# Macaron layer with a gated delta rule: POOL work moved to ScalarE, with new orders, stages and PSUM banks

## The chip, the core and the metric

The kernel runs on one core of one Trainium2 chip. The metric is the device time of one execution in microseconds. The engines are called PE (TensorE), DVE (VectorE), ACT (ScalarE), POOL (GpSimd) and SP (SyncE).

## What is computed

Input and output are 2 sequences of 4096 tokens with 256 channels, all float32. The layer is a feed-forward half step, a mixer, and the same feed-forward half step again:

```python
x = x + 0.5 * ffn(layernorm(x))
x = x + mixer(layernorm(x))
x = x + 0.5 * ffn(layernorm(x))

def ffn(x):                       # x_prev: the token before
    xr = mu_r * x + (1 - mu_r) * x_prev
    xk = mu_k * x + (1 - mu_k) * x_prev
    return sigmoid(xr @ W_r.T) * (square(relu(xk @ W_k.T)) @ W_v.T)

def mixer(h):                     # 16 heads of 16 channels
    q, k, v = (silu(conv4(h @ W.T)) for W in (Wq, Wk, Wv))
    q, k = l2norm(q) / 4, l2norm(k)
    beta, g = sigmoid(h @ Wb.T), -exp(A_log) * softplus(h @ Wa.T + dt_bias)
    for t in tokens:              # one 16x16 state per head
        S = S * exp(g[t])
        S = S + outer(k[t], (v[t] - k[t] @ S) * beta[t])
        o[t] = q[t] @ S
    return (rmsnorm(o) * norm_w * silu(h @ Wg.T)) @ Wo.T
```

## The kernel before

The 4096 tokens are cut into 32 groups of 128 tokens, both sequences together, so that a tile is 128 partitions by 512 columns. The recurrence is computed in chunks of 16 tokens: inside a chunk a triangular system is solved, and eight chunk steps (`chain`, n = 0 to 7) carry the state through a group.

The work of a group is split into some hundred segments, and a segment belongs to one engine. Each engine has its order of segments written out by hand in a loop `for step in range(GROUPS + 6)`, 38 steps. `on(segment, step - k)` runs a segment for group `step - k` if there is such a group, so that k is the stage at which the segment stands, and six to seven groups are in flight. An engine executes its list strictly in order; the engines wait for each other by semaphores. A segment of PE also waits until the PSUM bank that it writes is free. The table `PS` (L35) gives each product its bank, and the second to fourth `wait_ge` of a PE segment name the last reader of that bank.

The segments that matter here, with their lines:

- **DVE.** `stats1` to `stats3` (L1055, L1058) and `shift1` to `shift3` (L1241, L1187, L1319) belong to the layer norms. `mix_k1`, `mix_r1`, `mix_k3`, `mix_r3` mix a token with the one before (L1076, into XK and XR). `conv_q`, `conv_k`, `conv_v` (L1089) add three taps out of PSUM. `k_normed` (L1166) writes the normalised keys. `gram0` to `gram3` (L1346 to L1422) apply decays to Gram products and copy keys into KD (L1352, L1380, L1401, L1422). `solve_mul` and `solve_sub` (L1106, L1111) are the fifteen rows of the triangular solve, `t_turn` (L1147) turns the result. `chain` (L1127) copies the state out of PSUM, `o_turn` (L1135) and `o_merge` (L1141) collect outputs, `d_out0` to `d_out3` add products into Z2. `x1`, `x2`, `x3` (L1438 and L1439, L1269, L1174 and L1175) add to the residual.
- **PE.** `chain` (L408), `t_product`, `d_product0` to `3`, `gram0` to `3` (all through `pairs`, L251), the projections `q_proj`, `k_proj`, `v_proj` (L242) and `gate` (L476), `wo` and the feed-forward products (L226, L233), `turn1` to `turn3` (L219), `decay_steps` (L374), `decay_sums` (L418), `k_squares`, `o_squares` (L563, L571).
- **ACT.** Everything with a function table, and most copies out of PSUM. Functions come in two table sets; `ln_exp_set()` and `silu_set()` (L635, L638) load one, and each stands twice in a step. `exp_d` (L700) makes E from the sums of `decay_steps`; `t_out0`, `t_out1` (L852 to L862) write WP.
- **POOL.** Fourteen segments of whole-tile products and copies, among them `square1` and `square3` (L956, L960), `v_both` (L990), `q_slots` (L985), `t_start` (L1013), `q_decayed` (L979), `g_ident` (L951), `g_diag`, `e_mask` (L1017), `stat0`, `stat1`, `beta_diag`, `o_sum`, `gate_norm`.

Two examples, a segment with its waits and a piece of the order of POOL:

```python
def q_slots(g):
    pool.wait_ge(s["qe"], g + 1)
    if g:
        pool.wait_ge(s["mt"], 4 * g)
    tt(vw(GZ[:, :, C:], [2 * U, PACKS], [C, 2], [1, C]), vw(QE[:], [C, PACKS], [0, 2], [1, C]),
       vw(slot, [0, PACKS], [1, 2], [0, C]), ALU.mult).then_inc(s["qp"], 1)
...
    on(e_mask, step - 4)
    on(q_decayed, step - 4)
    on(q_slots, step - 4)
    on(g_ident, step - 4)
    on(t_start, step - 4)
```

Of the kernel before, what the change touches and what calls it, by code (L numbers as in the profile page):

```python
# [1589 lines left out]
```

## Time and profile before

| | us |
|---|---|
| median of 3 runs (lowest to highest) | 1776.21 (1775.66 to 1776.98) |
| the profiled execution | 1770.41 |
| its span, first to last instruction | 1768.4 |
| granted TensorE clock, mean, as a share of full | 0.913 |
| HBM read and written | 12.14 MB and 8.39 MB |

The page gives the busy time of each engine over the span. The trace behind it answers by line, by form, by stretch of time and by wait. Busy PE time includes time at a lower granted clock, and the idle time of an engine that isn't the bottleneck costs nothing. DMA is busy for a few per cent after the first slices.

### The profile page before, as it was taken

How to read it: one execution, taken by the hardware profiler on the slowest of the kernel's cores; microseconds unless marked ns; L12 is line 12 of the kernel's file. 1: busy time of each engine (PE TensorE's matmuls, PEld its weight loads, DVE VectorE, ACT ScalarE, POOL GpSimd, SP SyncE). 2: the span in 40 equal slices, each digit the busy share in tenths (PEclk: the TensorE clock that was granted, in tenths of full speed). 3: DMA queues.
4: the chain of work that ended last, by engine and by line, in shares of the span. 5: the costliest groups of instructions: out<-in, count | busy, mean ns of one | idle time of the engine just before them, and what ended most of it. 6: DMA issues, size and time to landing. Idle time of an engine off the chain costs nothing.

```text
span 1768.4 us, 92707 instructions
## 1 busy us (share of the span) xinstructions
PE 1519.7 (86%) x40960; PEld 1242.9 (70%) x40960; DVE 1530.0 (87%) x3975; ACT 1023.4 (58%) x1947; POOL 583.9 (33%) x453
## 2 busy tenths in 40 slices
PE   3878988988898898898988898898889888898875
PEld 2667776777777777777777777777777777776664
DVE  2889899889998988999999989989998999898662
ACT  6756566545656554656555566655565665556533
POOL 0333333234433323433333432423442333343301
PEclk8989999989998988998999899999898999898877
DMA  4000000000000000000000000000000000000000
GB/s 132 1 3 4 16 15 14 5 15 16 16 15 15 4 15 15 15 16 15 3 16 15 15 16 16 9 9 15 15 16 15 11 9 9 9 10 10 10 9 13
DMA packets 21839, 26.46 MB, mean 15 GB/s; under 512 B 2241, under 2 KB 20801, under 8 KB 21441
## 3 DMA queue, kind: packets, MB, share of 16 engines
q1 hardware_dynamic: 21440, 20.54, 3.6%
q8 instruction: 325, 5.32, 1.3%
q14 instruction: 74, 0.60, 0.1%
HBM read 12.14 MB, written 8.39 MB: 12 GB/s over the span
## 4 chain that ended last, share of the span: by engine, by line
DVE 46%; PE 31%; issue 14%; ACT 5%; DVEq 1%; POOL 1%; ACTq 0%; POOLq 0%
PE ps L233 11%; DVE CV L1089 6%; PE ps L242 5%; DVE XR L1076 4%; PE ps L251 4%; DVE TZ L1111 4%; PE ps L408 4%; DVE T L1147 3%; PE ps L476 3%; DVE KD L1352 3%; DVE st L1055 2%; DVE prod L1106 2%; DVE KD L1380 2%; ACT L635 2%; PE ps L392 2%
## 5 line engine op out<-in xcount | busy, mean ns | idle before, releaser
L408 PEld LDWEIGHTS ps<-MV,Z 32*32 32x32 f32 x16384 | 176.1, 112 | 192.6 <-DVE MV L1127 117.3
L408 PE MATMUL ps<-MV,Z 32*32 32x16 f32 x16384 | 203.2, 185 | 114.5 <-DVE MV L1127 96.3
L960 POOL TENSOR_TENSOR XK<-XK 128x512 f32<-128x512 f32 x32 | 38.9, 1215 | 635.3 <-ACT XK L799 635.3
L1089 DVE SCALAR_TENSOR_TENSOR CV<-ps,cw,CV 128x256 f32<-128x256 f32 x576 | 233.0, 475 | 5.9 <-ACT CV L681 5.9
L233 PE MATMUL ps<-w_v_ffn,XK 128*128 128x256 f32 x512 | 171.6, 493 | 4.2 <-DVE KD L1401 2.4
L251 PE MATMUL ps<-WP,KD 32*32 32x64 f32 x8192 | 148.4, 222 | 3.2 <-issue 2.0
L1111 DVE TENSOR_TENSOR TZ<-TZ,prod 128x30 f32<-128x30 f32 (+7 forms) x480 | 142.1, 296 | 6.9
L251 PEld LDWEIGHTS ps<-WP,KD 32*32 32x32 f32 x8192 | 128.9, 109 | 17.8 <-issue 13.0
L233 PEld LDWEIGHTS ps<-w_v_ffn,XK 128*128 128x128 f32 x512 | 119.1, 244 | 27.3 <-issue 3.0
L251 PEld LDWEIGHTS ps<-GK,T 32*32 32x32 f32 x8192 | 89.0, 108 | 69.2 <-issue 42.6
L251 PE MATMUL ps<-KQI,K 64*64 64x48 f32 x4096 | 133.2, 220 | 2.8 <-ACT K L632 2.7
L226 PE MATMUL ps<-XK,w_k_ffn 128*128 128x256 f32 x512 | 131.8, 403 | 2.5 <-DVE XK L1076 2.5
L233 PE MATMUL ps<-w_r_ffn,XR 128*128 128x256 f32 x512 | 128.6, 396 | 4.6 <-DVE XR L1076 3.3
L251 PEld LDWEIGHTS ps<-KQI,K 64*64 64x64 f32 x4096 | 125.1, 135 | 9.0 <-ACT K L632 2.8
L754 ACT ACTIVATE GS<-ps 128x512 f32<-128x512 f32 x32 | 19.1, 597 | 192.7 <-PE ps L476 192.6
L1106 DVE TENSOR_TENSOR prod<-A,TZ 128x30 f32<-128x30 f32 (+7 forms) x480 | 119.1, 248 | 10.1
L242 PE MATMUL ps<-YT,w_q 128*128 128x262 f32 x256 | 82.1, 475 | 49.8 <-DVE X L1175 49.8
L251 PE MATMUL ps<-GK,T 32*32 32x32 f32 x8192 | 106.0, 196 | 20.5 <-DVE T L1147 13.9
L1127 DVE COPY_PREDICATED MV<-pair,ps 128x128 f32<-128x128 uint32 x256 | 75.1, 293 | 50.9 <-PE ps L408 50.9
L233 PEld LDWEIGHTS ps<-w_r_ffn,XR 128*128 128x128 f32 x512 | 96.8, 199 | 17.2 <-DVE XR L1076 3.7
L226 PEld LDWEIGHTS ps<-XK,w_k_ffn 128*128 128x128 f32 x512 | 97.5, 200 | 15.9 <-issue 2.8
L1076 DVE SCALAR_TENSOR_TENSOR XR<-XR,mu,XT 128x256 f32<-128x256 f32 x128 | 108.3, 887 | 0.2 <-issue 0.2
(139 smaller groups left out, 3605.1 us busy)
## 6 DMA issues: line engine op xcount, KB each, us to landing
X<-in_x SPq DMA_DIRECT2D x32, 256.0 KB, 2.7
out_x<-X SPq DMA_DIRECT2D x32, 256.0 KB, 2.1
KQI<-in_blocks SPq DMA_DIRECT2D x2, 256.0 KB, 4.1
KD<-in_blocks SPq DMA_DIRECT2D x2, 256.0 KB, 4.6
w_r_ffn<-in_wT_r_ffn SPq DMA_DIRECT2D x1, 256.0 KB, 3.3
w_k_ffn<-in_wT_k_ffn SPq DMA_DIRECT2D x1, 256.0 KB, 3.6
w_v_ffn<-in_wT_v_ffn SPq DMA_DIRECT2D x1, 256.0 KB, 4.4
w_k<-in_wT_k SPq DMA_DIRECT2D x1, 256.0 KB, 4.3
```

What stands on the lines that cost most here:

```text
L226: last = mm(ps[:, dst * BANK + m * HB:dst * BANK + (m + 1) * HB], wt[:, k, m * P:(m + 1) * P], src[:, k * HB:(k + 1) * HB], start=(k == 0) ...
L233: last = mm(ps[:, dst * BANK + b * H:dst * BANK + (b + 1) * H], src[:, k * HB + b * TG:k * HB + (b + 1) * TG], wt[:, k, :], start=(k == 0) ...
L242: last = mm(ps[:, o:o + B * (CT + TG)], wt[:, k, m * P:(m + 1) * P], YT[:, k].rearrange("p b t -> p (b t)"), start=(k == 0), stop=(k == M ...
L251: last = mm(ps[rows, o:o + n], stat[rows, pk].rearrange("p s c -> p (s c)"), mov[rows], **flags)
L408: last = mm(ps[rows, o:o + C], Z2[g % 2][rows, pk, ab * U:(ab + 1) * U], MV[g % 2][rows, pk, ab, :], start=True, stop=True)
L476: last = mm(ps[:, o:o + HB], w["g"][:, k, m * P:(m + 1) * P], YT[:, k, :, CT:], start=(k == 0), stop=(k == M - 1))
L1076: last = stt(d3[:, rows], diff[:, rows], mu[:, kind, m:m + 1], XT[f][:, rows, 0:TG], ALU.mult, ALU.add)
L1089: stt(d4[:, m], src, cw[:, i, m, tap:tap + 1], d4[:, m], ALU.mult, ALU.add).then_inc(signal, 1)
L1106: tt(pr, a_j, t_j, ALU.mult).then_inc(s["sol"], 1)
L1111: tt(t_i, t_i, pr, ALU.subtract).then_inc(s["sol"], 1)
L1127: nc.vector.copy_predicated(state_rows_of(dst, m), vw(state_rows, [0, M * B], [1, U]), vw(src, [U, M * B], [1, U])).then_inc(s["ch_s"], 1)
L1147: nc.vector.transpose(vw(T2[:], [C, 2], [1, C], [U, PACKS]), vw(TZ[:], [2 * C * C, 2], [1, C], [C, U])).then_inc(s["tp"], 1)
```

## The change

Five segments move from POOL to ACT: `square1`, `square3`, `q_slots` (now two copies scaled by a mask column), `v_both` and `t_start`. The order of segments is written anew on PE, ACT, POOL and DVE, and many segments stand at another stage. Every product has its PSUM bank chosen anew, and the waits for banks on PE follow. ACT loads a table set six times per step. The arithmetic stays the same.

```diff
--- before.py
+++ after.py
@@ -32,9 +32,9 @@
 PAIR = U + 2 + HT + U
 AB0 = 320
 SOL = 2 * (C - 1)
-PS = {"xt1": 3, "yt": 0, "xt3": 0, "r1": 4, "k1": 6, "v1": 6, "r3": 0, "k3": 6, "v3": 5, "wo": 4, "g": 5,
-      "dd": 4, "eq": 1, "ssk": 3, "oss": 0, "gr0": 3, "d0": 1, "gr1": 1, "d1": 1, "gr2": 6, "d2": 1,
-      "gr3": 5, "d3": 0, "t0": 1, "t1": 6, "kc0": 3, "kc1": 4, "qc0": 5, "qc1": 2, "vc0": 2, "vc1": 4,
+PS = {"xt1": 4, "yt": 2, "xt3": 4, "r1": 3, "k1": 4, "v1": 4, "r3": 2, "k3": 3, "v3": 3, "wo": 1, "g": 6,
+      "dd": 3, "eq": 6, "ssk": 1, "oss": 4, "gr0": 6, "d0": 1, "gr1": 0, "d1": 6, "gr2": 4, "d2": 0,
+      "gr3": 6, "d3": 4, "t0": 4, "t1": 5, "kc0": 0, "kc1": 2, "qc0": 1, "qc1": 6, "vc0": 0, "vc1": 5,
       "ch": 7}
 
...
 def wo(g):
     pe.wait_ge(s["ot"], g + 1)
-    if g < GROUPS - 3:
-        pe.wait_ge(s["ck"], 6 * g + 24)
-        pe.wait_ge(s["tapk"], g + 4)
-    if g == GROUPS - 3:
-        pe.wait_ge(s["cv"], 6 * g + 18)
-        pe.wait_ge(s["tapv"], g + 3)
-    if g == GROUPS - 2:
-        pe.wait_ge(s["e"], g + 2)
+    if g < GROUPS - 1:
+        pe.wait_ge(s["mt"], 4 * g + 5)
     if g == GROUPS - 1:
         pe.wait_ge(s["x2"], g)
...
@@ q_proj @@
         pe.wait_ge(s["mix_in"], 16 * (len(MIX_IN) + 9))
     pe.wait_ge(s["yt"], g + 1)
     if g:
-        pe.wait_ge(s["cv"], 6 * g)
-        pe.wait_ge(s["tapv"], g)
-    if 1 <= g < 4:
         pe.wait_ge(s["gs"], g)
-    if g >= 4:
-        pe.wait_ge(s["x3"], g - 3)
+        pe.wait_ge(s["rnk"], g)
     conv_cols((PS["qc0"], PS["qc1"]), w["q"])
...
+def square1(g):
+    act.wait_ge(s["relu1"], g + 1)
+    af(KA[0][:], KA[0][:], ACT.Square).then_inc(s["ka1"], 1)
+
+def square3(g):
+    act.wait_ge(s["relu3"], g + 1)
+    af(KA[1][:], KA[1][:], ACT.Square).then_inc(s["ka3"], 1)
+
+def q_slots(g):
+    act.wait_ge(s["qe"], g + 1)
+    if g:
+        act.wait_ge(s["mt"], 4 * g)
+    own.done(af(GZ[:, :, C:2 * C], packs(QE[:]), ACT.Copy, scale=slot[:, 0:1]))
+    af(GZ[:, :, 2 * C:3 * C], packs(QE[:]), ACT.Copy, scale=slot[:, 1:2]).then_inc(s["qp"], 1)
+
+def v_both(g):
+    act.wait_ge(s["vt"], g + 1)
+    nc.scalar.copy(MV[g % 2][:, :, 1, :], MV[g % 2][:, :, 0, :]).then_inc(s["v2"], 1)
+
+def t_start(g):
+    if g == 0:
+        act.wait_ge(s["mix_in"], 16 * (len(MIX_IN) + 9))
+    if g:
+        act.wait_ge(s["tp"], g)
+    nc.scalar.copy(vw(TZ[:], [3 * C * C, 2], [1, C * C]),
+                   vw(t_one[:], [C * C, 2], [1, C * C])).then_inc(s["t_one_in"], 1)
+
```

The orders after the change, in short: `chain.2-5` is `on(chain, step - 5, 2)`, `mul` and `sub` are `solve_mul` and `solve_sub`.

```
PE: chain.2-5 k_squares-3 turn3-6 chain.3-5 v_proj-3 chain.4-5 turn1-1 turn2-2 chain.5-5 ffn3_k-6 chain.6-5 q_proj-2
  chain.7-5 ffn3_r-6 t_product.0-4 t_product.1-4 ffn3_v-6 t_product.2-4 t_product.3-4 k_proj-2 t_product.4-4
  t_product.5-4 t_product.6-4 o_squares-5 decay_sums-3 d_product0-4 t_product.7-4 ffn1_k-1 d_product1-4 d_product2-4
  decay_steps-3 gram0-3 d_product3-4 gram1-3 wo-5 gram2-3 chain.0-4 gram3-3 ffn1_r-1 chain.1-4 ffn1_v-1 gate-2
ACT: tap_q-3 o_square-6 norm1-1 t_out0-5 gates_wide-4 tap_k-3 ln_exp_set() o_root-6 halo3-6 exp_q-4 t_out1-5
  soft_exp-3 t_start-4 relu1-2 square1-2 v_both-5 exp_d-4 silu_set() silu_k-3 halo1-1 silu_v-4 square_k-3 ln_exp_set()
  rstd3-6 silu_set() silu_q-3 tanh1-2 q_slots-4 norm3-6 gate-3 ln_exp_set() rstd2-2 xt3-6 norm2-2 k_root-3 halo_y-2
  rstd1-0 yt-2 relu3-6 tap_v-3 square3-6 xt1-1 square_q-3 k_slots-3 o_first-5 silu_set() tanh3-6
POOL: g_ident-5 o_sum-6 stat0-4 stat1-4 q_decayed-4 gate_norm-6 g_diag-4 e_mask-4 beta_diag-3
DVE: d_out0-5 d_out1-5 d_out2-5 soft_low-3 o_norm-6 stats1-0 g_reduce-4 d_out3-5 gram0-4 chain.7-6 gram1-4 v_turn-4
  x2-6 gram2-4 stats3-6 chain.0-5 gram3-4 shift3-6 a_turn-4 chain.1-5 mul.0-4 o_turn.0-5 sub.0-4
  mul.1-4 sub.1-4 mul.2-4 soft_part-3 sub.2-4 x1-2 mul.3-4 sub.3-4 mul.4-4
  chain.2-5 sub.4-4 stats2-2 mul.5-4 sub.5-4 mul.6-4 chain.3-5 sub.6-4 o_turn.1-5
  mul.7-4 shift2-2 sub.7-4 mix_k3-6 chain.4-5 mul.8-4 sub.8-4 mul.9-4 sub.9-4
  o_turn.2-5 mul.10-4 chain.5-5 sub.10-4 soft_log-3 mul.11-4 sub.11-4 mul.12-4
  k_normed-3 sub.12-4 mul.13-4 chain.6-5 mix_r3-6 shift1-0 soft_max-3 sub.13-4 mul.14-4
  gates-3 sub.14-4 t_turn-4 o_turn.3-5 conv_v-3 o_merge-5 mix_k1-1 conv_q-2 gates_in-2 mix_r1-1 conv_k-2 x3-6
```

## Rows read from the trace of the kernel before

**Rows 1.** The page's busy time, share of the span and instructions of each engine.

```profile
PE 1519.7 (86%) x40960; PEld 1242.9 (70%) x40960; DVE 1530.0 (87%) x3975; ACT 1023.4 (58%) x1947; POOL 583.9 (33%) x453
```

**Rows 2.** Stretch 400 to 1400 us: time; PE, PEld, DVE, ACT, POOL busy; clock; DMA share; GB/s.

```profile
400.00:1400.00 1000.00, 891.53 (x24399) 731.07 (x24397) 917.84 (x2360) 588.76 (x1145) 351.31 (x269) 0.93 0.05 13
```

**Rows 3.** Line L1439 in that stretch: duration ns min/median/max, first and last start us.

```profile
L1439 DVE SCALAR_TENSOR_TENSOR X<-XR,X x19: 691/692/694, 439.2 to 1386.6; 128x512 f32<-128x512 f32 x19
```

**Rows 4.** Groups by form, DVE: operation xcount | busy us, mean ns | idle before.

```profile
L1076 DVE SCALAR_TENSOR_TENSOR XR<-XR,mu,XT 128x256 f32<-128x256 f32 x128 | 108.3, 887 | 0.2 <-issue 0.2
...
L1076 DVE SCALAR_TENSOR_TENSOR XK<-XR,mu,XT 128x256 f32<-128x256 f32 x128 | 57.2, 488 | 2.3
...
L1166 DVE TENSOR_TENSOR KQI<-CV,SK 128x512 f32<-128x512 f32 x32 | 50.5, 1577 | 0.0
L1352 DVE COPY_PREDICATED KD<-pair,KE 128x256 f32<-128x256 uint32 x32 | 48.7, 1523 | 0.0
L1380 DVE COPY_PREDICATED KD<-pair,KE 128x256 f32<-128x256 uint32 x32 | 42.3, 1323 | 0.0
...
L1319 DVE SCALAR_TENSOR_TENSOR nmr<-mv,rstd 128x2 f32<-128x2 f32 x32 | 35.6, 1112 | 0.6 <-ACT rstd L627 0.6
...
L1422 DVE COPY_PREDICATED KD<-pair,KE 128x256 f32<-128x256 uint32 x32 | 13.9, 435 | 0.0
...
L1241 DVE SCALAR_TENSOR_TENSOR nmr<-mv,rstd 128x2 f32<-128x2 f32 x32 | 5.7, 179 | 14.8 <-ACT rstd L627 14.8
```

**Rows 5.** Timeline, 848 to 852 us, DVE and POOL: start us, us, engine, line, operation.

```profile
848.14 1.26 POOL L979 TENSOR_TENSOR QE<-KQI,EQ 128x512 f32<-128x512 f32 x1
848.20 1.22 DVE L1319 SCALAR_TENSOR_TENSOR nmr<-mv,rstd 128x2 f32<-128x2 f32 x1
...
849.48 1.89 POOL L985 TENSOR_TENSOR GZ<-QE,pair 128x1024 f32<-128x1024 f32 x1
...
850.08 1.60 DVE L1352 COPY_PREDICATED KD<-pair,KE 128x256 f32<-128x256 uint32 x1
```

**Rows 6.** Waits from 400 to 1400 us: who waited for whom, total us, times, longest us.

```profile
PE ps L408 <- DVE MV L1127: 57.8, 19, 3.3
...
PE ps L242 <- DVE X L1175: 36.2, 19, 2.0
...
DVE MV L1127 <- PE ps L408: 24.1, 14, 1.9
```

**Rows 7.** Stretch 804 to 806.5 us, columns as in the second group.

```profile
804.00:806.50 2.50, 2.50 (x7) 1.55 (x5) 1.78 (x5) 0.00 (x0) 0.00 (x0) 0.50 0.00 0
```

**Rows 8.** Timeline of PE, then DVE, 800 to 852 us; in brackets the idle time before.

```profile
802.85 3.78 PE L233 MATMUL ps<-w_v_ffn,XK 128*128 128x256 f32 x8
...
807.68 0.30 DVE L1127 COPY_PREDICATED MV<-pair,ps 128x128 f32<-128x128 uint32 x1 [1.87 <-PE ps L408]
...
824.72 1.99 PE L233 MATMUL ps<-w_v_ffn,XK 128*128 128x256 f32 x8
```

**Rows 9.** Groups by form, POOL: the five operations that leave it, xcount | busy us, mean ns.

```profile
L985 POOL TENSOR_TENSOR GZ<-QE,pair 128x1024 f32<-128x1024 f32 x32 | 60.8, 1899 | 2.5
...
L960 POOL TENSOR_TENSOR XK<-XK 128x512 f32<-128x512 f32 x32 | 38.9, 1215 | 635.3 <-ACT XK L799 635.3
L956 POOL TENSOR_TENSOR XK<-XK 128x512 f32<-128x512 f32 x32 | 38.5, 1204 | 39.4 <-ACT XK L722 39.4
L1013 POOL COPY TZ<-t_one 128x512 f32<-128x512 f32 x32 | 25.8, 805 | 0.0
L990 POOL COPY MV<-MV 128x512 f32<-128x512 f32 x32 | 19.5, 609 | 96.5 <-DVE MV L1445 96.5
```

**Rows 10.** Groups by form, ACT: table loads of one set, a square, a masked copy out of PSUM.

```profile
L635 ACT ACT_TABLE_LOAD x77 | 98.8, 1283 | 1.9 <-DVE prod L1455 0.6
...
L861 ACT ACTIVATE WP<-ps,pair 128x512 f32<-128x512 f32 x32 | 21.9, 685 | 64.8 <-PE ps L251 64.8
...
L786 ACT ACTIVATE SK<-CV 128x512 f32<-128x512 f32 x32 | 19.7, 614 | 0.2
```

More of the change, by code:

```diff
@@ L447, in turn3 @@
                     pe.wait_ge(s["ro"], g + 1)
+                if g < GROUPS - 4:
+                    pe.wait_ge(s["x1"], g + 5)
                 turn(PS["xt3"], XN[2], s["xt3_ps"])
@@ L575, in _ @@
             for step in range(GROUPS + 6):
-                on(chain, step - 5, 0)
+                on(chain, step - 5, 2)
+                on(k_squares, step - 3)
                 on(turn3, step - 6)
-                on(ffn1_r, step - 2)
-                on(chain, step - 5, 1)
-                on(ffn1_v, step - 2)
-                on(chain, step - 5, 2)
-                on(gate, step - 3)
                 on(chain, step - 5, 3)
+                on(v_proj, step - 3)
+                on(chain, step - 5, 4)
                 on(turn1, step - 1)
-                on(ffn3_r, step - 6)
-                on(chain, step - 5, 4)
-                on(v_proj, step - 3)
+                on(turn2, step - 2)
                 on(chain, step - 5, 5)
@@ L912, in _ @@
                 on(o_root, step - 6)
-                on(k_slots, step - 4)
+                on(halo3, step - 6)
+                on(exp_q, step - 4)
                 on(t_out1, step - 5)
-                on(tap_q, step - 3)
+                on(soft_exp, step - 3)
+                on(t_start, step - 4)
+                on(relu1, step - 2)
+                on(square1, step - 2)
+                on(v_both, step - 5)
+                on(exp_d, step - 4)
+                silu_set()
+                on(silu_k, step - 3)
                 on(halo1, step - 1)
-                on(exp_d, step - 4)
-                on(rstd1, step - 1)
+                on(silu_v, step - 4)
+                on(square_k, step - 3)
+                ln_exp_set()
                 on(rstd3, step - 6)
-                on(norm3, step - 6)
-                on(xt3, step - 6)
-                on(soft_exp, step - 3)
                 silu_set()
@@ L1027, in _ @@
             for step in range(GROUPS + 6):
-                on(square1, step - 2)
+                on(g_ident, step - 5)
+                on(o_sum, step - 6)
+                on(stat0, step - 4)
+                on(stat1, step - 4)
+                on(q_decayed, step - 4)
                 on(gate_norm, step - 6)
-                on(v_both, step - 4)
+                on(g_diag, step - 4)
                 on(e_mask, step - 4)
-                on(q_decayed, step - 4)
-                on(q_slots, step - 4)
-                on(g_ident, step - 4)
-                on(t_start, step - 4)
-                on(square3, step - 6)
-                on(g_diag, step - 3)
-                on(stat0, step - 3)
-                on(o_sum, step - 5)
                 on(beta_diag, step - 3)
-                on(stat1, step - 3)
         @block.vector
@@ L1458, in _ @@
             for step in range(GROUPS + 6):
-                on(g_reduce, step - 4)
-                on(d_out1, step - 5)
-                on(gates_in, step - 3)
+                on(d_out0, step - 5)
+                on(d_out1, step - 5)
+                on(d_out2, step - 5)
+                on(soft_low, step - 3)
+                on(o_norm, step - 6)
+                on(stats1, step)
+                on(g_reduce, step - 4)
+                on(d_out3, step - 5)
+                on(gram0, step - 4)
+                on(chain, step - 6, 7)
+                on(gram1, step - 4)
+                on(v_turn, step - 4)
                 on(x2, step - 6)
-                on(conv_q, step - 3)
-                on(d_out2, step - 5)
+                on(gram2, step - 4)
                 on(stats3, step - 6)
-                on(d_out3, step - 5)
-                on(shift3, step - 6)
-                on(gram0, step - 4)
-                on(gram1, step - 4)
-                on(gram2, step - 4)
-                on(shift1, step - 1)
-                on(gram3, step - 4)
                 if step == 5:
```

328 lines of the change are left out of this document (165 added, 163 removed).

## The prediction

> **What bounds the kernel now.** I read the page's busy shares first [rows 1]: DVE and PE are both near 87%, ACT at 58%, POOL at 33%. A share over the whole span hides fill and drain, so next comes the steady stretch [rows 2] and its period. One DVE line runs once for each group of tokens; it started 19 times from 439.2 to 1386.6 us [rows 3], so the period is 947.4 / 18 = 52.6 us. In 1000 us there are 19.0 periods. Per period [rows 2] DVE is busy 917.84 / 19 = 48.3 us, PE 46.9, ACT 31.0, POOL 18.5. DVE idles only 4.3 us. It is the bound, with PE close behind.
>
> How much of the 48.3 us is work? The by-form groups answer it [rows 4]: instructions of one shape have very different means. The second copy into KD takes 1323 ns where the fourth, the same shape, takes 435. The timeline shows why [rows 5]: a DVE shift of 2 columns starts 0.06 us after a POOL product, takes 1.22 us, and ends as that product does. The next KD copy starts inside POOL's 1.89 us masked copy and ends just after it. So some DVE instructions stand still until POOL's current instruction is done. Those hit read two SBUF tensors. The price of it [rows 4]: mix of XR 128 x (887 - 488) = 51.1 us; normalised keys 32 x (1577 - 692) = 28.3, taking 692 from a 512-wide line that is never hit [rows 3]; KD copies 32 x (1523 - 435) + 32 x (1323 - 435) = 63.2; shift 32 x (1112 - 179) = 29.9. Sum 172.5 us, 5.4 per group. DVE's own work is then 48.3 - 5.4 = 42.9 us.
>
> The waits close the picture [rows 6]. Once a period PE waits up to 3.3 us for the chain's copy on DVE, which is late because the stretch before it (decayed Gram products) holds the blocked KD copies and shift. A second wait, up to 2.0 us, is that of the query projection for the residual sum on DVE. After the first wait the granted clock is 0.50, the 1.2 GHz level [rows 7]: the same eight matmuls take 3.78 us where they take 1.99 later, and DVE then idles 1.87 us at the next chain copy [rows 8]. That is how 4.3 us of DVE idle arise: lost time on DVE makes PE wait, the wait costs PE its clock, and DVE waits in turn.
>
> **The change part by part.** *Leaves POOL:* masked query copies 1899 ns, squares 1204 and 1215, start rows 805, second values 609 [rows 9], together 5.7 us per group, so POOL goes from 18.5 to 12.8. What DVE gets back depends on which of its instructions POOL meets. In proportion, 5.4 x 12.8 / 18.5 = 3.7 us stay, 1.7 are saved. Bounds: 1 us stays if the new order keeps POOL under single-input work, 6 if every remaining instruction blocks something.
>
> By the new lists POOL's decay products and g_ident come behind beta_diag, which is released by gates, while DVE runs t_turn and conv_v (one SBUF tensor in each); e_mask stays just ahead of gram0; and nothing of POOL is due during gram0 to gram3, where 2.9 us of the 5.4 were lost (KD copies 63.2 us and shift 29.9 over 32). Against that, beta_diag now meets the end of the solve, o_sum meets mix_k1, and stat0 and stat1 meet mix_r1: three or four meetings of about 1.2 us. Both readings give some 3.7 us, and I take it. DVE: 42.9 + 3.7 = 46.6 us per period.
>
> *Arrives at ACT:* two squares at 614 ns, two masked copies at 685, two plain copies at about 614 [rows 10]: 3.8 us. ACT also gets six table loads per step in place of four. Now one of the two lines that load shows 77 = 2 x 38 + 1 of 1283 ns [rows 10], the other one has as many but the one at the start; two more per step are 2.6 us, 76 x 1283 ns = 97.5 us in all. ACT goes from 31.0 to 37.4 us of the period. It is not the bound; this stands beside DVE work and I cost it at nothing. If the cover goes (a period under 38 us, or a wait queued ahead of exp_d) it costs what it lacks.
>
> The Trainium skill (ScalarE: Activation LUTs, section "Table sets: the hidden batching unit") reckons a switch of table set at about 2.7 us; by that the 76 more loads would be an estimated 205 us and ACT some 40 us per period, still below DVE. The trace's duration is half of it and decides.
>
> *New PSUM banks and order:* no instruction is added or removed on PE or DVE. The new waits fall mostly on work of an earlier group. The query projection leaves its place behind x3 and now follows chain step 6 and waits for gs and rnk of the group before, so the second PE wait has no cause left. The first has: chain step 0 still needs d_out3, and step 1 the copy of step 0, with gram3 and ffn1_r between. Behind it now stand ffn1_v and gate, two blocks of about 2 us that at the lower clock take 3.8 each [rows 8]. DVE has about 4 us of its own between its copies 1 and 2 (an estimate: x1 with two lines of some 692 ns, an output transpose and ten short solve steps). So an idle of up to some 2.6 us can return at chain copy 2. DVE idle now 4.3; bounds 0.5 (PE never cold) to 5 (cold as now, longer blocks); I take 2.0, the old 4.3 less the part behind the projection.
>
> *Sum.* Period 46.6 + 2.0 = 48.6 us, 4.0 less. Of 38 steps 27 have every stage; the thin ones together I count as one more: 28 x 4.0 = 113 us. The profiled execution took 1770.4 us, 5.8 less than the 1776.2 median of the runs. 1776.2 - 113 = **1663 us**. Its own range, with period 47.1 to 50.1, is 1621 to 1706.
>
> **Rivals.**
>
> *A. The blocking nearly vanishes.* DVE 42.9 + 1.5 and 1.6 idle give 46.0; PE must fit: 46.9 us busy at a mean clock of 0.93 [rows 2] is about 43.2 at full clock (14% of the time at half). 28 x 6.6 = 185 us, 1591. For: gram0 to gram3 are free of POOL. Against: three meetings remain, and PE and DVE with 43 us each leave little play. 0.13.
>
> *B. The blocking only moves.* The rows show that whichever starts first runs to its end, and the other one waits. Then removing 5.7 us of POOL work need not free a proportionate share: a POOL instruction released just ahead of a two-input DVE instruction costs its full length. With 4.7 of the 5.4 us left and the longer cold blocks keeping idle at 3.9, the period is 42.9 + 4.7 + 3.9 = 51.5: 28 x 1.1 = 31 us, 1745. 0.18. The Trainium skill says the same (SBUF — State Buffer, section "Who interferes with whom"): a DVE instruction with two SBUF inputs and a GpSimd one that reads SBUF exclude each other for a whole instruction, by issue order. By that rule, the trace agrees: 1.22 us for a shift of 2 columns.
>
> *C. Slower: ACT becomes the late one at exp_d.* On its in-order list exp_d now stands behind a table load, o_root, exp_q, t_out1, soft_exp, t_start, relu1, square1 and v_both. t_out1 waits for the last triangular product. From its start to exp_d are at least 2 x 685 + 4 x 614 ns = 3.8 us, soft_exp's five small steps not counted, where before it stood behind t_out1, tap_q and halo1 only. Behind it wait e_mask, then gram0 on DVE with the whole chain. It decides from the point where ACT reaches exp_d more than about 1 us after decay_steps; then POOL's e_mask and what follows also slide back under the Gram stretch. Price: blocking back at 5.4 us, idle 2.0 + 3.7: 42.9 + 5.4 + 5.7 = 54.0, 28 x 1.4 = 39 us more, 1815. For: ACT rises by 6.4 us and each table load holds all behind it. Against: ACT still has 11 us to spare at 48.6, and decay_steps too has moved ahead of the Gram products. 0.15.
>
> *D. Nothing changes,* gains and losses cancel within 0.2% (about what a measurement of this kernel can tell from no change): 1776. 0.03.
>
> **How the numbers follow.** Forecast 0.51, A 0.13, B 0.18, C 0.15, D 0.03. Faster by over 0.2%: 0.51 + 0.13 + 0.18 = 0.82. Same 0.03, slower 0.15. The range runs from A's value to that of no change, 1590 to 1776: half of A's chance lies below it and most of C's above, together 2 in 10.
>
> **What would show it.** In the profile of the changed kernel: the period, from the starts of x1's last line, near 48.6; POOL busy about 583.9 - 183.5 = 400 us, no POOL instruction inside gram0 to gram3; all four KD copies near 435 ns; the shift near 180; XR mix still above 488; the query projection without a wait for DVE; 153 + 76 = 229 table loads; ACT busy about 1240 us; clock above 0.93. The prediction is wrong if KD copies stay above 1 us (B), if DVE waits at gram0 for POOL's E behind ACT's exp_d (C), or if PE stays above 2.4 us of waits per period for the chain copy with ffn1_v and gate at the low clock.

## The result and the profile after

The changed kernel takes 1549.05 us (median of 4 runs, 1546.72 to 1550.92); the kernel before took 1776.6 (median of 4 beside them, 1775.66 to 1792.74). The ratio on record is 0.87, 95% interval 0.8649 to 0.8751; the quotient of the two medians, 0.872, lies inside it. That is 227.6 us less, where 113 were forecast. The time lies 41 us below the lower end of the range.

The page's busy times and shares of the span (1548.8 us) answer to [rows 1]:

```profile
PE 1443.1 (93%) x40960; PEld 1183.5 (76%) x40960; DVE 1383.2 (89%) x3975; ACT 1219.2 (79%) x2215; POOL 396.9 (26%) x293
```

A stretch of whole periods answers to [rows 2], same columns (time; PE, PEld, DVE, ACT, POOL busy; clock):

```profile
401.20:1294.10 892.90, 882.46 (x25602) 725.56 (x25601) 863.32 (x2481) 728.29 (x1361) 247.90 (x180) 1.00 0.05 16
```

The line that gave the period [rows 3] is L1453 now:

```profile
L1453 DVE SCALAR_TENSOR_TENSOR X<-XR,X x21: 691/692/693, 401.2 to 1294.1; 128x512 f32<-128x512 f32 x21
```

It started 21 times in 892.9 us: the period is 892.9 / 20 = 44.65 us, 8.0 less than 52.6, where 4.0 less was forecast. The count of periods held: 28 x 8.0 = 224 us of the 227.6. Per period PE is busy 882.46 / 20 = 44.1 us, DVE 43.2, ACT 36.4, POOL 12.4. PE has 0.5 us to spare and its granted clock is 1.00: PE, no longer DVE, is the fullest engine, and it loses no clock in the steady stretch. Below, e4 shows that DVE stands right behind it.

The waits of PE in the stretch 400 to 1300 us (total, times, longest) hold no wait for the chain copy nor for the residual sum, which were 3.3 and 2.0 us at the longest [rows 6]. The longest that another engine causes is 0.4 us, once:

```profile
PE ps L418 <- DVE Z L1316: 0.4, 1, 0.4
```

The two blocks behind the chain steps, `ffn1_v` and `gate`, run at full clock, where `ffn1_v` took 3.78 us before [rows 8]:

```profile
709.42 1.99 PE L233 MATMUL ps<-w_v_ffn,XK 128*128 128x256 f32 x8
711.25 1.89 PE L480 MATMUL ps<-YT,w_g 128*128 128x256 f32 x8
```

The DVE groups by form (busy us, mean ns, over the whole run) answer to [rows 4]. The second KD copy (L1394) fell from 1323 to 437 ns, the first from 1523 to 478, the shift from 1112 to 153, the keys from 1577 to 692. The mix of XR only went from 887 to 731, and the mix of XK rose from 488 to 699:

```profile
L1090 DVE SCALAR_TENSOR_TENSOR XR<-XR,mu,XT 128x256 f32<-128x256 f32 x128 | 88.5, 731 | 0.1
L1090 DVE SCALAR_TENSOR_TENSOR XK<-XR,mu,XT 128x256 f32<-128x256 f32 x128 | 84.2, 699 | 2.3
...
L1180 DVE TENSOR_TENSOR KQI<-CV,SK 128x512 f32<-128x512 f32 x32 | 22.1, 692 | 2.5 <-ACT SK L849 2.3 <-issue 0.3
...
L1366 DVE COPY_PREDICATED KD<-pair,KE 128x256 f32<-128x256 uint32 x32 | 15.3, 478 | 0.0
...
L1394 DVE COPY_PREDICATED KD<-pair,KE 128x256 f32<-128x256 uint32 x32 | 14.0, 437 | 0.0
...
L1125 DVE TENSOR_TENSOR TZ<-TZ,prod 128x30 f32<-128x30 f32 x64 | 11.7, 183 | 0.1
...
L1333 DVE SCALAR_TENSOR_TENSOR nmr<-mv,rstd 128x2 f32<-128x2 f32 x32 | 4.9, 153 | 1.0 <-ACT rstd L638 1.0
```

The timeline of POOL and DVE over one period (start, us) shows where POOL's work stands now. Ahead of `beta_diag` (724.98) POOL is idle for 24.15 us, over the whole Gram stretch; its list goes on while DVE convolves, and then meets both mixes:

```profile
724.98 1.06 POOL L1022 TENSOR_TENSOR LD<-cz,msk 128x512 f32<-128x512 f32 x1 [24.15 <-DVE cz L1233]
...
730.99 1.96 DVE L1090 SCALAR_TENSOR_TENSOR XK<-XR,mu,XT 128x256 f32<-128x256 f32 x2
...
731.40 1.27 POOL L1002 TENSOR_TENSOR OSQ<-OSQ,SQ 128x512 f32<-128x512 f32 x1 [3.43 <-ACT OSQ L843]
...
735.41 1.61 POOL L1033 TENSOR_TENSOR ST<-ST,LD 128x512 f32<-128x512 f32 x1
735.42 1.88 DVE L1090 SCALAR_TENSOR_TENSOR XR<-XR,mu,XT 128x256 f32<-128x256 f32 x2
```

`o_sum` starts inside the mix of XK, and `stat1` starts 0.01 us before the mix of XR. ACT's table loads in the steps stand under two lines, 229 in all (one more comes ahead of the steps):

```profile
L649 ACT ACT_TABLE_LOAD x115 | 147.5, 1283 | 2.5 <-DVE prod L1469 0.6
L646 ACT ACT_TABLE_LOAD x114 | 146.3, 1283 | 2.0
```

### The profile page after: what moved, and what is told of

It is laid out like the page before. It is cut to its first block, busy times and chain, and to the rows that moved or that the text cites. A ratio compares the mean times of both kernels' runs of the same rounds, so it can differ in the third digit from the quotient of the medians.

```text
span 1548.8 us, 92755 instructions
## 1 busy us (share of the span) xinstructions
PE 1443.1 (93%) x40960; PEld 1183.5 (76%) x40960; DVE 1383.2 (89%) x3975; ACT 1219.2 (79%) x2215; POOL 396.9 (26%) x293
## 4 chain that ended last, share of the span: by engine, by line
issue 72%; POOL 21%; ACT 3%; PE 2%; DVE 1%; POOLq 0%; ACTq 0%; DVEq 0%
POOL GZ L996 4%; POOL GD L1042 3%; POOL OSQ L1002 3%; POOL ST L1033 3%; POOL E L1036 3%; POOL ST L1028 3%; POOL GS L1009 2%; ACT L649 1%; ACT L646 1%; PE ps L226 0%; PE ps L242 0%; POOL QE L1016 0%; PE ps L233 0%; POOL LD L1022 0%; PE ps L251 0%
## 5 line engine op out<-in xcount | busy, mean ns | idle before, releaser
L1022 POOL TENSOR_TENSOR LD<-cz,msk 128x512 f32<-128x512 f32 x32 | 33.9, 1060 | 815.5 <-DVE cz L1233 815.5
L404 PEld LDWEIGHTS ps<-MV,Z 32*32 32x32 f32 x16384 | 164.9, 107 | 75.2 <-issue 55.5
L404 PE MATMUL ps<-MV,Z 32*32 32x16 f32 x16384 | 190.4, 181 | 18.1 <-DVE MV L1141 9.2
L251 PE MATMUL ps<-KQI,K 64*64 64x48 f32 x4096 | 148.1, 221 | 4.4 <-issue 3.4
L649 ACT ACT_TABLE_LOAD x115 | 147.5, 1283 | 2.5 <-DVE prod L1469 0.6
L646 ACT ACT_TABLE_LOAD x114 | 146.3, 1283 | 2.0
L251 PE MATMUL ps<-WP,KD 32*32 32x64 f32 x8192 | 138.6, 215 | 6.8 <-issue 5.6
L636 ACT ACTIVATE lnv<-mv,headp 128x2 f32<-128x2 f32 x96 | 28.3, 294 | 131.5 <-DVE mv L1072 131.5
L233 PE MATMUL ps<-w_v_ffn,XK 128*128 128x256 f32 x512 | 127.2, 391 | 0.4 <-ACT XK L910 0.4
L1125 DVE TENSOR_TENSOR TZ<-TZ,prod 128x30 f32<-128x30 f32 (+7 forms) x480 | 119.8, 250 | 6.9
L233 PEld LDWEIGHTS ps<-w_v_ffn,XK 128*128 128x128 f32 x512 | 92.2, 189 | 13.1 <-ACT XK L910 0.8
L251 PE MATMUL ps<-GK,T 32*32 32x32 f32 x8192 | 96.9, 194 | 3.8 <-issue 2.1
L1141 DVE COPY_PREDICATED MV<-pair,ps 128x128 f32<-128x128 uint32 x256 | 74.1, 289 | 19.4 <-PE ps L404 18.5
```

The lines of the kernel that those rows point to most:

```text
L233: last = mm(ps[:, dst * BANK + b * H:dst * BANK + (b + 1) * H], src[:, k * HB + b * TG:k * HB + (b + 1) * TG], wt[:, k, :], start=(k == 0) ...
L251: last = mm(ps[rows, o:o + n], stat[rows, pk].rearrange("p s c -> p (s c)"), mov[rows], **flags)
L404: last = mm(ps[rows, o:o + C], Z2[g % 2][rows, pk, ab * U:(ab + 1) * U], MV[g % 2][rows, pk, ab, :], start=True, stop=True)
L646: nc.scalar.preload_act_table_set("natural_log_exp_and_others")
L649: nc.scalar.preload_act_table_set("silu_and_others")
L1125: tt(t_i, t_i, pr, ALU.subtract).then_inc(s["sol"], 1)
```

## The experiments

Two things had to be told apart. First, what took the time: POOL blocking DVE instructions that read two SBUF tensors, or late POOL results, or the order. Second, why the period fell by twice the forecast. The table gives each run per period, in us: the busy share of the stretch 400 to 1300 us times the period. A count over whole periods, as the text uses in places, differs by up to 0.3; DVE of the kernel before is such a count. The last column is the ratio on record to the kernel before run beside it (medians there 1773.7 to 1778.5).

| kernel | period | PE busy | DVE busy | ACT busy | POOL busy | clock | median us | ratio (95%) |
|---|---|---|---|---|---|---|---|---|
| before | 52.6 | 46.9 | 48.2 | 31.1 | 18.5 | 0.93 | 1776.6 | 1 |
| changed | 44.65 | 44.1 | 43.2 | 36.4 | 12.3 | 1.00 | 1549.05 | 0.870 (0.865 to 0.875) |
| e1 before, POOL one column | 44.2 | 43.5 | 41.3 | 30.9 | 1.7 | 1.00 | 1534.95 | 0.865 (0.861 to 0.868) |
| e13 changed, POOL one column | 44.5 | 44.0 | 41.0 | 36.3 | 0.8 | 1.00 | 1543.10 | 0.869 (0.863 to 0.875) |
| e9 before, POOL fills only | 44.5 | 43.5 | 41.8 | 30.9 | 15.1 | 1.00 | 1548.70 | 0.873 (0.867 to 0.879) |
| e2 before, five segments moved | 47.6 | 44.7 | 44.8 | 34.2 | 12.0 | 0.98 | 1640.96 | 0.924 (0.919 to 0.928) |
| e15 before, `q_slots` moved | 50.7 | 45.9 | 47.1 | 32.1 | 16.1 | 0.95 | 1713.43 | 0.965 (0.959 to 0.972) |
| e3 changed, segments back on POOL | 46.4 | 44.6 | 45.0 | 33.1 | 17.5 | 1.00 | 1599.43 | 0.900 (0.896 to 0.905) |
| e8 before, POOL's list alone | 47.2 | 43.9 | 45.4 | 30.8 | 17.8 | 1.00 | 1638.89 | 0.925 (0.921 to 0.930) |
| e10 before, e2 and a list like e8's | 49.0 | 44.9 | 46.9 | 34.3 | 12.3 | 0.98 | 1679.32 | 0.945 (0.940 to 0.951) |
| e7 before, more PE work | 50.9 | 46.7 | 48.1 | 30.7 | 18.5 | 0.97 | 1724.87 | 0.973 (0.967 to 0.980) |
| e4 changed, less PE work | 44.3 | 43.4 | 42.9 | 36.3 | 12.4 | 1.00 | 1544.31 | 0.870 (0.866 to 0.873) |
| e5 changed, 2 POOL products, Gram | 44.7 | 44.2 | 43.3 | 36.4 | 14.3 | 1.00 | 1548.46 | 0.874 (0.870 to 0.878) |
| e11 changed, 4 POOL products, Gram | 44.5 | 44.0 | 43.3 | 36.4 | 16.6 | 1.00 | 1547.66 | 0.871 (0.866 to 0.876) |
| e6 changed, 2 POOL products, conv | 44.8 | 44.1 | 43.2 | 36.4 | 14.3 | 1.00 | 1555.03 | 0.878 (0.874 to 0.881) |
| e12 changed, 4 POOL products, conv | 49.0 | 45.9 | 45.3 | 36.4 | 17.3 | 0.95 | 1672.62 | 0.942 (0.936 to 0.947) |
| e14 changed, 2 more table loads | 46.4 | 44.7 | 43.6 | 39.0 | 12.1 | 0.99 | 1608.99 | 0.906 (0.898 to 0.914) |

### What POOL's work costs

**e1** keeps every wait and signal of POOL in the kernel before. From group 2 on it leaves the computation of POOL's products and of its copy of the values out and sets one column in the place of each; `t_start` stays. The heart of the edit:

```diff
-            tt = nc.gpsimd.tensor_tensor
+            full = nc.gpsimd.tensor_tensor
...
+            def tiny():
+                used[0] += 1
+                return nc.gpsimd.memset(few[:, used[0]:used[0] + 1], 0.0)
+
+            def tt(dst, a, b, op):
+                if now[0] < 2:
+                    return full(dst, a, b, op)
+                return tiny()
```

> The kernel before with every tensor product of POOL, and its copy of the values, replaced from group 2 on by the setting of one column, each under the waits and signals it had (t_start stays). It leaves that part of the computation out. Theory 1, the blocking of two-input DVE instructions and what follows from it (PE waits, low clock, DVE idle) is the whole difference between the two kernels: the period falls from 52.6 us to 45 or 46, 1776 - 28 x 7 = 1580 us, all four KD copies near 435 ns, clock above 0.96. Theory 2, the new order is what counts: only the 5 to 6 us of blocking go and the waits of PE stay, half of it or less reaches the period: 1690 us or more.

Measured: 1534.95 us, 45 below what theory 1 expected, and the old order with PE at full clock. The stretch of 19 periods:

```profile
440.50:1279.70 839.20, 827.13 (x24368) 685.23 (x24356) 784.54 (x2357) 584.62 (x1142) 32.20 (x266) 1.00 0.05 16
```

DVE's own work is 784.54 / 19 = 41.3 us, against 866.75 / 18 = 48.2 in the kernel before: POOL's blocking was 6.9 us a period. The rows below are DVE's by form over whole steady periods, first of the kernel before, then of e1:

```profile
L1076 DVE SCALAR_TENSOR_TENSOR XR<-XR,mu,XT 128x256 f32<-128x256 f32 x72 | 64.0, 929 | 0.0
...
L1166 DVE TENSOR_TENSOR KQI<-CV,SK 128x512 f32<-128x512 f32 x18 | 31.4, 1742 | 0.0
...
L1352 DVE COPY_PREDICATED KD<-pair,KE 128x256 f32<-128x256 uint32 x18 | 28.9, 1607 | 0.0
L1380 DVE COPY_PREDICATED KD<-pair,KE 128x256 f32<-128x256 uint32 x18 | 23.9, 1330 | 0.0
L1111 DVE TENSOR_TENSOR TZ<-TZ,prod 128x30 f32<-128x30 f32 x36 | 22.4, 622 | 0.0
L1319 DVE SCALAR_TENSOR_TENSOR nmr<-mv,rstd 128x2 f32<-128x2 f32 x18 | 21.7, 1205 | 0.0
```

```profile
L1097 DVE SCALAR_TENSOR_TENSOR XR<-XR,mu,XT 128x256 f32<-128x256 f32 x76 | 33.3, 481 | 0.0
...
L1187 DVE TENSOR_TENSOR KQI<-CV,SK 128x512 f32<-128x512 f32 x19 | 13.2, 693 | 0.0
...
L1373 DVE COPY_PREDICATED KD<-pair,KE 128x256 f32<-128x256 uint32 x19 | 8.4, 442 | 0.0
...
L1132 DVE TENSOR_TENSOR TZ<-TZ,prod 128x30 f32<-128x30 f32 x38 | 7.4, 194 | 0.0
```

XR mix 4 x (929 - 481) = 1.8 us, KD copies 1.2 + 0.9, shift 1.05 (its mean in e1 is 154 ns), keys 1.05, and the last `sub` of the solve 2 x (622 - 194) = 0.85: 6.8 of the 6.9.

**e13** is the same edit on the changed kernel.

> The changed kernel with every POOL product from group 2 on replaced by the setting of one column (that part of the computation is left out). DVE's blocking, 1.9 us a group by now, goes. Theory 1, PE at full clock is the floor of both kernels: the time is that of the old order without blocking, 1530 to 1545 us. Theory 2, the 1.9 us that are left still cost their length: 1549 - 28 x 1.9 = 1496 us.

```profile
400.00:1300.00 900.00, 888.38 (x25889) 734.79 (x25888) 829.06 (x2512) 734.51 (x1376) 17.00 (x180) 1.00 0.05 16
```

1543.10 us, against 1549.05: the intervals of the two ratios overlap almost wholly, so this is theory 1. DVE falls from 870.01 to 829.06 us, over whole periods by 2.1 us per period, and the period goes from 44.65 to 44.5 only, with PE busy 44.0 of it. The blocking left in the changed kernel is both mixes, 4 x (750 - 477) and 4 x (736 - 482) = 2.1 us, by its own steady rows and e13's:

```profile
L1090 DVE SCALAR_TENSOR_TENSOR XR<-XR,mu,XT 128x256 f32<-128x256 f32 x80 | 56.8, 750 | 0.0
L1090 DVE SCALAR_TENSOR_TENSOR XK<-XR,mu,XT 128x256 f32<-128x256 f32 x80 | 55.6, 736 | 1.4
```

```profile
L1111 DVE SCALAR_TENSOR_TENSOR XK<-XR,mu,XT 128x256 f32<-128x256 f32 x80 | 35.2, 482 | 1.4
...
L1111 DVE SCALAR_TENSOR_TENSOR XR<-XR,mu,XT 128x256 f32<-128x256 f32 x80 | 34.9, 477 | 0.0
```

**e9** asks whether it is POOL's being busy, or late, that costs, or its reads. From group 2 on each product becomes a fill of about its length and a fill of one column, which read nothing, and the copy of the values a shorter fill; that part of the computation is left out. The heart of the edit, with a function `fill` that two others call:

```diff
+            def fill(cols):
...
+                nc.gpsimd.memset(few[k % 3][:, 0:cols], 0.0).then_inc(s["fills"], 1)
+                return nc.gpsimd.memset(tick[:, k:k + 1], 0.0)
+
+            def tt(dst, a, b, op):
+                if now[0] < 2:
+                    return full(dst, a, b, op)
+                return fill(1280)
```

> The kernel before with every tensor product of POOL, from group 2 on, replaced by a fill of 1280 columns of a spare tile (about 1.2 us by the 0.95 us of the 1024-column fill at the start) and a one-column fill, its copy of the values by a shorter fill; waits and signals stay. It leaves that part of the computation out. POOL is then busy nearly as long as before but reads nothing from SBUF. Theory 1, DVE's two-input instructions wait because POOL reads SBUF: they run free and the time is that of the run with tiny POOL work, 1535 to 1560 us. Theory 2, that run was faster because POOL's results came sooner (latency of e_mask, stat1, o_sum): the time stays at 1700 or more. Theory 3, writing blocks too: KD copies above 1 us, 1740 or more.

1548.70 us with POOL busy 15.1 us per period, where it was 18.5. The timeline shows copies into KD taking 0.45 and 0.44 us though a fill of some 1.16 us starts inside each of them (at 699.71 and 700.85), and, in the same stretch, one that takes 0.86 us because POOL's only operation that still reads SBUF (the start rows) began 0.05 us before it:

```profile
699.61 0.45 DVE L1378 COPY_PREDICATED KD<-pair,KE 128x256 f32<-128x256 uint32 x1
699.71 1.16 POOL L955 MEMSET few<- 128x1280 f32 x1
...
700.83 0.44 DVE L1406 COPY_PREDICATED KD<-pair,KE 128x256 f32<-128x256 uint32 x1
...
701.99 0.61 POOL L1039 COPY TZ<-t_one 128x512 f32<-128x512 f32 x1
702.04 0.86 DVE L1427 COPY_PREDICATED KD<-pair,KE 128x256 f32<-128x256 uint32 x1
```

The time lies 14 us above that of e1, with ratios whose intervals overlap, and DVE is still busy 0.4 us longer per period than in e1, since the start rows go on reading. So POOL results that come late are at most a small part of the 228 us; POOL's reads are the cause. The Trainium skill (SBUF — State Buffer, section "Who interferes with whom") says that a DVE instruction with two SBUF inputs contends with a GpSimd one that reads SBUF and not with one that only writes it: these rows agree.

### Moves against places

**e2** puts the five segments on ACT in the kernel before, with its orders and banks kept (added lines of ACT's list, the comments are mine):

```diff
+                on(square1, step - 2)   # ACT, behind relu1
+                on(v_both, step - 4)    # behind t_out1
+                on(t_start, step - 4)
+                on(q_slots, step - 4)   # behind soft_exp
+                on(square3, step - 6)   # behind relu3
```

> The kernel before in its own order and banks, with only the five segments moved from POOL to ACT (squares behind their relus, v_both and t_start behind t_out1, q_slots behind soft_exp), four table loads as before. Theory 1: the Gram stretch of DVE still has POOL's e_mask, q_decayed and g_ident on top of it, so some 2 to 3 us of blocking a period go (the KD copies that met q_slots and t_start, squares on mixes): 1776 - 28 x 2.5 = 1706 us, between 1680 and 1740. Theory 2, the moves bring the gain: below 1620. Theory 3, they bring nothing without the order: 1765 or more.

**e3** does the opposite: the changed kernel with the five segments back on POOL, `t_start` and `v_both` behind `o_sum`, `square1`, `q_slots` and `square3` behind `e_mask`.

> The changed kernel in its new order and banks, with the five segments back on POOL (t_start and v_both behind o_sum; square1, q_slots and square3 behind e_mask, thus under the Gram stretch of DVE), six table loads kept. Theory 1, place of POOL's work: square1 and q_slots (1.2 and 1.9 us) block KD copies again, the chain is late, PE waits and loses its clock: period from 44.7 to 48 or 49, 1549 + 28 x 4 = 1660 us, 1630 to 1700. Theory 2, the order alone is the gain: 1549 to 1565.

**e8** leaves every operation on POOL and changes three places of its list:

```diff
                 on(v_both, step - 4)
+                on(q_decayed, step - 4)
                 on(e_mask, step - 4)
-                on(q_decayed, step - 4)
-                on(q_slots, step - 4)
-                on(g_ident, step - 4)
                 on(t_start, step - 4)
                 on(square3, step - 6)
+                on(g_ident, step - 4)
+                on(q_slots, step - 4)
```

> The kernel before with all its POOL work, banks and other orders, only three POOL segments moved within POOL's own list: q_decayed ahead of e_mask, g_ident and q_slots behind square3 (which waits for relu3 and so starts at the end of the solve). Theory 1: the KD copies and the third shift are free, about 3 us of blocking and its knock-on go, while the later POOL list meets mixes and keys: 1776 - 28 x 4 = 1664 us, 1620 to 1700. If the moves to ACT were needed for any gain: 1765 or more.

Against the medians beside them, the moves alone (e2) give 138 us (ratio 0.924), the new orders, stages and banks alone, with the six table loads, (e3) 179 (0.900), both 228 (0.870). I had expected less of either, 1706 and 1660 us. The two don't add up: both take blocking away, and with the blocking gone e1 and e13 stop at 44.2 and 44.5 us. e8 is the surprise: with 17.8 us of POOL work per period it takes 135 us off, about as much as e2 with 12.0. Over the run its first two KD copies take 532 and 491 ns, the shift 493, the keys 792; only the mix of XR is left at 874. What matters is which DVE instruction POOL's list meets, not how much POOL does. In e3 the first KD copy meets `q_slots` and takes 1707 ns (mean over the run), longer than before's 1523, and the period is still 6 us shorter.

**e10** joins e2 with the places of e8 (`q_decayed` ahead of `e_mask`, `g_ident` released near the end of the solve).

> The old orders and banks with both cures: the five segments on ACT, and in POOL's list q_decayed ahead of e_mask and g_ident held until the end of the triangular solve. All of the computation is there. Alone the moves gave 1641 and the new places 1639 us. Theory 1, both only take blocking away and PE at full clock is the floor (43.5 to 44.1 us a period): 1776 - 28 x 7 = 1580 us, 1555 to 1600. Theory 2, the new order of PE, DVE and ACT and the banks hold a gain of their own: 1620 or more here, against 1549.

It takes 1679.32 us, worse than either, and theory 1 is refuted. The timeline (brackets: idle before) shows why. `g_ident` starts 0.21 us before the mix's difference, which then takes 2.31 us (685 ns in e1), `g_diag` holds the mix of XK, `stat0` holds a step of the solve (1.27 us), and PE waits 2.05 us for XK:

```profile
726.06 1.97 POOL L984 TENSOR_TENSOR GZ<-pair,EQ 128x1024 f32<-128x1024 f32 x1 [20.65 <-DVE TZ L1118]
...
726.27 2.31 DVE L1291 TENSOR_TENSOR XR<-XT 128x512 f32<-128x512 f32 x1
...
728.61 1.89 DVE L1083 SCALAR_TENSOR_TENSOR XK<-XR,mu,XT 128x256 f32<-128x256 f32 x2
...
728.87 1.35 POOL L1035 TENSOR_TENSOR GD<-EQ,msk 128x512 f32<-128x512 f32 x1 [0.84 <-ACT EQ L708]
...
730.55 3.68 PE L226 MATMUL ps<-XK,w_k_ffn 128*128 128x256 f32 x8 [2.05 <-DVE XK L1083]
```

Theory 2 had given 1620 or more, for a gain that the new orders hold of their own. With e1 and e13 beside it, that gain is in what POOL's list meets, and no other is to be seen.

**e15** moves only `q_slots`, behind `soft_exp` on ACT.

> The kernel before with only the masked query copies moved to ACT (behind soft_exp). Theory 1, the 1.9 us POOL product under the Gram stretch is the most harmful of the five: g_ident and t_start come 1.9 us sooner and end before the later KD copies, some 1 to 2 us of blocking go: about 1776 - 28 x 2 = 1720 us, 1690 to 1745, more than half of what all five moves gave (1641). If each move counts by its own length (1.9 of 5.7 us): 1776 - 135 x 0.33 = 1731 us; no more than 1765 if it is the squares that count.

It gains 61 us (1713.43), less than half of the 138 of all five moves, where I had expected more than half. The second KD copy falls from 1323 to 521 ns over the run, DVE by 1.1 us per period and the period by 1.95: each microsecond of blocking was worth nearly two here.

### Why a microsecond of DVE is worth more than one

**e7** adds to the kernel before: the matmuls of `ffn1_r` are issued twice, which puts 1.9 us of PE work ahead of PE's wait for the chain copy.

```diff
+                for b in range(B):
+                    for k in range(M):
+                        mm(ps[:, PS["r1"] * BANK + b * H:PS["r1"] * BANK + (b + 1) * H],
+                           XR[0][:, k * HB + b * TG:k * HB + (b + 1) * TG], w["r_ffn"][:, k, :], start=(k == 0), stop=(k == M - 1))
                 rows_out(PS["r1"], w["r_ffn"], XR[0], s["r1_ps"])
```

> The kernel before with the r product of the first feed-forward (8 matmul passes, 1.9 us) computed twice in a row on PE, ahead of the wait for the chain's copy, where PE idles 3.3 us a period. It adds work and computes the same. If the low clock after that wait is part of the knock-on: PE idles only 1.4 us there, ffn1_v takes 2.0 us and not 3.8, DVE does not idle at the next copy, and in spite of more work the kernel gets faster: 1776 - 28 x 1.5 = 1734 us, 1700 to 1765. If the clock costs nothing because PE has slack: 1774 to 1780 us, or more by up to 28 x 1.9 = 53 us if the added work isn't covered.

With more work the kernel takes 1724.87 us, 2.7% less than before. DVE's busy time is the same, 48.1 us. PE's timeline shows the chain step behind a wait of 1.60 us where it was up to 3.3, and then `ffn1_v` in 1.99 us where it took 3.78 [rows 8]:

```profile
734.53 0.73 PE L408 MATMUL ps<-MV,Z 32*32 32x16 f32 x64 [1.60 <-DVE MV L1131]
735.18 1.99 PE L233 MATMUL ps<-w_v_ffn,XK 128*128 128x256 f32 x8
```

The added work only fills time in which PE was idle, so the gain of 49 us is that of the clock: the half clock behind PE's wait was on the path, and it was worth about a fifth of the 228 us.

**e4** leaves out half of the `gate` product on the changed kernel (`for k in range(1)`).

> The changed kernel with the second half of the gate product left out on PE (4 of 8 matmul passes, 0.95 us a group). If PE at full clock (44.1 us busy of a 44.65 us period) is now the bound, with DVE busy 43.2 behind it: the period falls by 0.5 to 0.9 us, 1549 - 28 x 0.7 = 1529 us, 1520 to 1536. If DVE or ACT sets the period and PE only fills it: no change, 1546 to 1552.

PE's work falls by 0.7 us and the period by 0.3, where I had expected 0.5 to 0.9 or nothing; the ratio, 0.870, is the same. So PE is not the only limit: with 0.7 us taken off PE, or 2.1 off DVE (e13), the other one holds the period. That the two share the bound is argued from these runs; no run takes from both at once. ACT's list has little play as well, as e14 will show.

### What play the changed kernel has left

**e5**, **e11**, **e6** and **e12** add POOL products that read SBUF and that nobody waits for (`tt(DUM[i], t_one, t_one, mult)`, some 1.1 us each): two and four behind `e_mask`, under the Gram products; two and four behind `beta_diag`, ahead of `g_ident` (e5 with e11, e6 with e12).

> The changed kernel plus two POOL products a group (each 512 columns, SBUF in, SBUF out, 1.27 us, result unused), placed right behind e_mask, so that they fall under gram0 and gram1 of DVE. Theory 1, the place of POOL's work sets the price: the first KD copies wait 1.5 to 2 us a group, DVE's busy time rises by as much, and nothing covers it: 44.65 -> 46.2 to 47 us, 1549 + 28 x 1.9 = 1602 us, 1585 to 1620. Theory 2, POOL's work beside a full PE costs nothing: 1549 to 1555.

> The changed kernel with four added POOL products a group behind e_mask in place of two (1.02 us each as the last run showed, where both were over before the second KD copy). Now they reach over gram0 to gram2. Theory 1: the first three KD copies wait 0.3 to 1 us each, 1.5 to 2.5 us a group, DVE goes to about 45 us of work: 1549 + 28 x 1.5 = 1591 us, 1570 to 1615. Theory 2: no more than 1555.

> The same two POOL products, placed behind beta_diag instead, so that they fall under t_turn and conv_v of DVE, which read one SBUF tensor each. Theory 1: no DVE instruction waits for them, 1549 to 1556 us. If the amount of POOL's work counts and not its place: the same 1600 us as in the run with them under the Gram stretch.

> The same four products behind beta_diag, under t_turn and conv_v. DVE's instructions there read one SBUF tensor. They also hold g_ident and o_sum back by up to 4 us, which the list covers for the most part: Theory 1: 1555 to 1575 us, less than with the four under the Gram stretch. If the amount and not the place counts: the same as there.

Neither two nor four products in the Gram stretch cost anything (e5 1548.46 us, e11 1547.66), where theory 1 had 1602 and 1591. The four run from 700.10 to 704.58, yet of the KD copies inside them the first takes 0.73 us and the second 0.43 (means over the run 721 and 435 ns):

```profile
700.10 4.48 POOL L1048 TENSOR_TENSOR DUM<-t_one 128x512 f32<-128x512 f32 x4
...
701.72 0.73 DVE L1377 COPY_PREDICATED KD<-pair,KE 128x256 f32<-128x256 uint32 x1
...
703.27 0.43 DVE L1405 COPY_PREDICATED KD<-pair,KE 128x256 f32<-128x256 uint32 x1
```

Two ahead of `g_ident` cost 6 us (e6), with ratios whose intervals overlap; four cost 124, where I had expected 6 to 26. They delay POOL's list by 4 us, and what stood under the convolution now falls on the mixes:

```profile
732.75 4.03 POOL L1048 TENSOR_TENSOR DUM<-t_one 128x512 f32<-128x512 f32 x4
...
736.75 2.41 POOL L997 TENSOR_TENSOR GZ<-pair,EQ 128x1024 f32<-128x1024 f32 x1
737.25 2.45 DVE L1309 TENSOR_TENSOR XR<-XT 128x512 f32<-128x512 f32 x1
...
739.12 1.72 POOL L1003 TENSOR_TENSOR OSQ<-OSQ,SQ 128x512 f32<-128x512 f32 x1
...
739.74 2.82 DVE L1101 SCALAR_TENSOR_TENSOR XK<-XR,mu,XT 128x256 f32<-128x256 f32 x2
```

PE then waits 3.0 us at the longest for the next chain operand, 19 times, and its clock falls to 0.95:

```profile
PE ps L419 <- DVE Z L1327: 54.7, 19, 3.0
```

**e14** adds two table loads per step to ACT, ahead of `halo3`:

```diff
                 on(o_root, step - 6)
+                silu_set()
+                ln_exp_set()
                 on(halo3, step - 6)
```

> The changed kernel with eight table loads a step in place of six (both sets loaded once more behind o_root, ahead of exp_q, 2.6 us). If ACT's work is covered, as costed: 1549 to 1556 us. If ACT's list is by now as tight as PE's (79% busy): exp_q, t_out1 and exp_d come 2.6 us late, 1549 + 28 x 1.5 = 1591 us or more. A half of that at 1556 to 1575 says that the lists have about 1 us of play.

ACT is busy 39.0 of 46.4 us and yet 2.6 us more on it cost 1.8 us of every period, 60 us in all (1608.99); for a list as tight as PE's I had given 1591 or more. The waits (total, times, longest) show the path: a product on PE waits for EQ, which `exp_q` writes on ACT, and Z on DVE waits for a product of that line:

```profile
DVE Z L1268 <- PE ps L251: 17.1, 20, 3.4
...
PE ps L251 <- ACT EQ L719: 15.5, 20, 1.0
```

## Why the prediction was wrong

The direction, the mechanism and the count of periods were right; the size was half. The signs came: no POOL instruction inside the Gram products, KD copies at 478, 437, 428 and 436 ns, the shift at 153, POOL busy 397 us. What failed is the sum for DVE, 42.9 + 3.7 = 46.6 us per period: both terms were too large, and 43.2 was measured. Step by step:

- **The blocking before, 5.4 us per group: too small.** It measured 6.9. Two faults in the sum. I took means over all 32 groups, the thin steps at both ends among them, where nothing is blocked: 887 for the XR mix where the steady mean is 929, 1523 for the KD copy where it is 1607. And I summed five groups only: the last `sub` of the solve (564 ns over the run, 183 after) was in nobody's list. So **DVE's own work, 42.9 us, is 41.3**, 1.6 too much.
- **The blocking that stays, 3.7 us: 2.1.** I took it by proportion to POOL's busy time and by counting three or four meetings at some 1.2 us each. Two came, `o_sum` with the mix of XK and `stat1` with the mix of XR, at about 1 us each. `beta_diag` did not hold the end of the solve (the last `sub` takes 183 ns), and `stat0` was over (734.04 + 1.29 us) before the mix of XR started at 735.42. e8 shows that proportion is no measure: all of POOL's work kept, 135 us gained.
- **DVE idle, 2.0 us: 1.5.** PE goes into the chain without a wait and ffn1_v and gate run at full clock.
- Together 1.6 + 1.6 + 0.5 = 3.7 of the 4.0 us by which the period is shorter than forecast; the last 0.3 is DVE's own work in the new order, 41.0 in e13 where e1 has 41.3. The sum as measured: 41.0 + 2.1 + 1.5 = 44.6. The factor 28 held, though 26 steps have every stage (6 to 31) and not 27. The lower end of the sum's own range, at 47.1 us, comes to 1622 and not 1621.
- **ACT "at nothing": right here, but its cover was not 11 us.** ACT's busy time came out as reckoned, 1219 us against some 1240, with 229 loads. But e14 shows less than a microsecond of play in its list at that place. A busy share does not show that; the waits behind `exp_q` do. The rival C (ACT late at `exp_d`) did not come: `e_mask` starts when the copy of E is ready and is over (700.83) before the Gram products start at 701.87.
- **Rival A** (the blocking nearly vanishes, 1591) was nearest, and it too carried the 42.9. It put PE's need at full clock at 43.2 us; the runs that compute all of PE's work at full clock show 43.5 to 44.1, and the kernel stands close to that.
- **Rival B** (blocking only moves) describes e10 and e12, not this change: there POOL's list falls on the mixes. The order of the changed kernel avoids it but for 2.1 us.

So the gain comes from DVE's blocking, 4.8 us less of it per period, and from what hung on it. DVE's busy time fell by 48.2 - 43.2 = 5.0 us and its idle time, with PE's waits and half clock gone, by 4.4 - 1.5 = 2.9; together they make the 8.0 but for rounding. With POOL's blocking gone both orders reach nearly the same time (e1 1535, e13 1543, the intervals overlap), so no gain of the new banks and order beyond it is to be seen. None of the runs that compute everything beats the changed kernel by more than its spread.
